# Ten rounds written out as straight code in place of a loop with six passes

## The chip, the cores and the metric

The kernel runs on one core of a Trainium2 chip. The metric is the device time of one execution, in microseconds. The core has five instruction streams that run side by side: TensorE (PE in the profile; its weight loads are listed apart as PEld), VectorE (DVE), ScalarE (ACT), GpSimd (POOL) and SyncE (SP), which here only starts transfers. They wait for one another through semaphores. A name with a q behind it (DVEq, PEldq) is the part of an engine that handles instructions before the work proper: register arithmetic, branches, waits, starts of transfers.

## The reference

The input x has 8 x 2048 tokens of 256 numbers, all float32. A layer norm is followed by a linear attention without a softmax, then a second layer norm and a mixture of experts with a short convolution:

```python
x = x + attn(layernorm(x), wq, wk, wv, wo)       # context = Q (K^T V) * sqrt(3/64), out = context wo^T, per sequence
x2 = layernorm(x)
scores = sigmoid(x2 @ Wr)                        # 8 experts
_, idx = top_k(scores + router_bias, 2)
w = scores[idx] / (sum + 1e-09)                  # spread over 8 columns as cw
hid = silu(x2 @ Wg[e]) * (x2 @ Wu[e])            # e = 0..3
routed = sum_e cw[:, e] * (hid @ Wd[e]) + (cw[:, 4] + cw[:, 6]) * x2 + cw[:, 7] * relu(x2)
x = x + routed + conv4(x2) + conv_b
```

## The kernel before

The 16384 tokens are 32 groups of 512 tokens (four tiles of 128), four groups to a sequence. Every group passes through stages, and each stage works on another group at the same time. One **step** of the program does stage L (load and first norm) for group s, stage A (transposes, and the Gram matrix of the normed rows) for group s-1, B (attention output, residual, second norm) for s-5, R (router) for s-6, C (experts) for s-7, and Y (output) for s-8; the table `LAG` holds these distances. A **round** is four steps, ten rounds are 40 steps, numbered 0 to 39 here. In the second step of a round stage B begins a new sequence, and a chain of small products (`ps_gram`, lines 518 to 545) folds the Gram matrix into one 256 x 256 matrix. Each product of the experts and of the attention is made as three matmuls of split operands (lines 371 to 373).

The order in each engine's stream is written by hand in its `body(st)`. The class `Step` decides which stages are on in a step and computes the number that each wait needs (`before`). The function `steps` calls `body`: rounds 0 and 1 and rounds 8 and 9 are written out with constants (*peeled*). Rounds 2 to 7, where all stages are on, are one copy of four steps in a hardware loop (`Fori`, line 295) with the round number in a register; the numbers for waits are then computed on each engine by register instructions. SyncE's loop ends one round earlier. Every engine goes through its own loop, and there is no barrier at a round's end.

Places of which the prediction speaks: in DVE's body line 938 (or 936) copies three columns ahead of the transposed group, the first VectorE work of a step; line 803 is the convolution, line 898 makes `x2T_lo`. TensorE's router matmuls (line 476) wait for `x2T_lo`, and TensorE works strictly in the order written. POOL's line 1059 is the router's exponential, line 1042 scales an expert's gate. PE's line 511 transposes the router's weights once in each step with stage R (steps 6 to 37), late in the step. The instructions of the loop itself all carry line 295.

Of the kernel before, what the change touches and what calls it, by code (L numbers as in the profile page):

```python
# [33 lines left out]
LAG = {"I": -1, "L": 0, "A": 1, "X": 4, "B": 5, "R": 6, "C": 7, "Y": 8}  # L34
UNROLL = 4
# [4 lines left out]
class Step:  # L40


    def __init__(self, r, s, groups):
        self.r, self.s, self.groups = r, s, groups
        self.peeled = isinstance(r, int)

    def on(self, stage):

        return not self.peeled or 0 <= UNROLL * self.r + self.s - LAG[stage] < self.groups

    def was_on(self, stage):


        return not self.peeled or 0 <= UNROLL * self.r + self.s - 1 - LAG[stage] < self.groups

    def later(self, stage, n):

        return not self.peeled or UNROLL * self.r + self.s - LAG[stage] >= n

    def first(self, stage):  # L60

# [10 lines left out]

    def before(self, stage, per=1, extra=0):

        n = self.s - LAG[stage]
        if self.peeled:
            return per * min(max(UNROLL * self.r + n, 0), self.groups) + extra
        return self.r * (UNROLL * per) + (n * per + extra)

    def uses(self, stage, n, per=1, extra=0):  # L80

# [3 lines left out]
    def chains(self, per=1, extra=0):  # L85


        k = (self.s - LAG["B"] - 1) // UNROLL + 1
        if self.peeled:
            return per * min(max(self.r + k, 0), self.groups // UNROLL) + extra  # L90
        return self.r * per + (k * per + extra)

    def chain(self):
        return self.first("B") and self.on("B")
# [6 lines left out]
def program(nc, x, wq, wkT, wvT, woT, wr, rbias, wg, wu, wd, convwb, cw_rows, out):  # L101
    T, H = x.shape
    D = wq.shape[0]
    NE = wr.shape[1]
    EM, _, I = wg.shape
    KC = convwb.shape[1] - 1
    HC = H // P
    TG = 4
    GT = TG * P
    NG = T // GT  # L110
    SCALE = math.sqrt(3.0 / D)
    assert D == 64 and I == P and HC == 2 and NG % UNROLL == 0
    ROUNDS = (NG + max(LAG.values())) // UNROLL
    LOOP = (LAG["Y"] // UNROLL, NG // UNROLL)

    x_rows = x.rearrange("(n p) f -> p n f", p=P)
    out_rows = out.rearrange("(n p) f -> p n f", p=P)
# [2 lines left out]
    with ctx:  # L120
# [166 lines left out]
        N_LOADS = 7 + 2 * EM + 1  # L287
        NSPLIT = 3

        def steps(eng, body, stop=LOOP[1]):  # L290

            for r in range(LOOP[0]):
                for s in range(UNROLL):
                    body(Step(r, s, NG))
            with eng.Fori(LOOP[0], stop, 1) as r:
                for s in range(UNROLL):
                    body(Step(r, s, NG))
            for r in range(stop, ROUNDS):
                for s in range(UNROLL):
                    body(Step(r, s, NG))  # L300

# [3 lines left out]
        @block.sync  # L305
        def _(sp):
            def load_x(st):

                if st.later("I", 2):
                    sp.wait_ge(xn_ready, st.before("I", TG, -TG))  # L310
                sp.dma_start(xa[:, st.slot("I", 2)], x_rows[:, bass.ds(st.group("I") * TG, TG), :])\
                    .then_inc(xa_loaded[st.slot("I", 2)], 16)

            load_x(Step(0, -1, NG))
            load_x(Step(0, 0, NG))
            sp.dma_start(wq_sb[:, :], wq).then_inc(w_loaded, 16)
            sp.dma_start(wkT_sb[:, :, :], wkT.rearrange("(c p) d -> p c d", p=P)).then_inc(w_loaded, 16)
            sp.dma_start(wvT_sb[:, :, :], wvT.rearrange("(c p) d -> p c d", p=P)).then_inc(w_loaded, 16)
            sp.dma_start(woT_sb[:, :], woT).then_inc(w_loaded, 16)
            sp.dma_start(wr_sb[:, :, :], wr.rearrange("(c p) e -> p c e", p=P)).then_inc(w_loaded, 16)  # L320
            sp.dma_start(conv_w[:, :, :], convwb.rearrange("(c p) k -> p c k", p=P)).then_inc(w_loaded, 16)
            sp.dma_start(bias8[:, :], rbias.partition_broadcast(P)).then_inc(w_loaded, 16)
            for e in range(EM):
                sp.dma_start(wg_st[:, e], wg[e].rearrange("(c p) i -> p c i", p=P)).then_inc(w_loaded, 16)
                sp.dma_start(wu_st[:, e], wu[e].rearrange("(c p) i -> p c i", p=P)).then_inc(w_loaded, 16)
            sp.dma_start(wd_st, wd.rearrange("e i n -> i e n")).then_inc(w_loaded, 16)

            def body(st):
                if st.on("I") and not (st.peeled and st.group("I") < 2):
                    load_x(st)  # L330
                if st.on("Y"):

                    k = st.slot("Y", 4)
                    for h in range(2):
                        sp.wait_ge(out_ready, st.before("Y", 2, h + 1))
                        sp.dma_start(out_rows[:, bass.ds(st.group("Y") * TG + 2 * h, 2), :],
                                     acc[:, k, 2 * h:2 * h + 2]).then_inc(out_stored[k], 16)
                if st.on("R"):

                    k = st.slot("R", 2)  # L340
                    rows = cw_rows[bass.ds(st.group("R"), 1)]
                    sp.wait_ge(cwT_ready, st.before("R", 1, 1))
                    sp.dma_start(rows.rearrange("a e (t n) -> (a e t) n", t=TG), cwT[:, :]).then_inc(cw_stored, 16)
                    sp.wait_ge(cw_stored, st.before("R", 16, 16))


                    if st.peeled and st.before("R") < 2:
                        sp.wait_ge(whi_ready, NSPLIT)
                        sp.wait_ge(wlo_ready, NSPLIT)
                    sp.dma_start(cwb[:, k].rearrange("p e n -> p (e n)"),  # L350
                                 rows.rearrange("a e n -> (a e n)").partition_broadcast(P))\
                        .then_inc(cwb_loaded[k], 16)
                if st.on("X"):

                    k = st.slot("X", 4)
                    if st.later("X", 4):
                        sp.wait_ge(out_stored[k], st.uses("X", 4, 32))
                    sp.dma_start(acc[:, k], x_rows[:, bass.ds(st.group("X") * TG, TG), :])\
                        .then_inc(acc_loaded[k], 16)

            steps(sp, body, LOOP[1] - 1)
            for k in range(4):
                sp.wait_ge(out_stored[k], 32 * (NG // 4))
            sp.wait_ge(cw_stored, 16 * NG)
# [3 lines left out]
        def _(pe):  # L368
# [182 lines left out]
            def body(st):  # L551
                c_on, y_on, r_on, a_on, b_on, m_on = (st.on("C"), st.on("Y"), st.on("R"), st.on("A"), st.on("B"),
                                                      st.chain())
                if st.peeled and b_on and st.before("B") == 0:
                    pe.wait_ge(w_loaded, 16 * N_LOADS)
                if st.peeled and c_on and st.before("C") == 0:
                    pe.wait_ge(wlo_ready, NSPLIT)
                if c_on:
                    gate_up(st, 0)
# [53 lines left out]
                if a_on and r_on:  # L613
                    xn_transpose(st, 1)

            steps(pe, body)


        @block.scalar
        def _(act):  # L620
# [36 lines left out]
            def split_weights():  # L657
                act.wait_ge(w_loaded, 16 * N_LOADS)
                copy(wgu_hi[:, 0].rearrange("p e c i -> p (e c i)"), wg_st.rearrange("p e c i -> p (e c i)"))\
                    .then_inc(whi_ready, 1)  # L660
                copy(wgu_hi[:, 1].rearrange("p e c i -> p (e c i)"), wu_st.rearrange("p e c i -> p (e c i)"))\
                    .then_inc(whi_ready, 1)
                copy(wd_hi[:, :, :], wd_st).then_inc(whi_ready, 1)
# [26 lines left out]

            def body(st):
                c_on, r_on, m_on = st.on("C"), st.on("R"), st.chain()
                if st.peeled and st.group("L") == LAG["B"] - 1:
                    split_weights()
                if m_on:
                    chain_copy(st, gram_done, st.before("A"),
# [67 lines left out]
                if st.on("B"):  # L764
                    norm2(st)

            steps(act, body)


        @block.vector  # L770
        def _(dve):
# [152 lines left out]

            def body(st):
                c_on, y_on, r_on, b_on, m_on = st.on("C"), st.on("Y"), st.on("R"), st.on("B"), st.chain()
                if st.peeled and st.group("L") == LAG["B"]:
                    split_weights()
                if r_on:
                    q = st.slot("R", 2)  # L930
# [38 lines left out]
                if c_on:  # L969

                    dve.wait_ge(relu_ready, st.before("C", TG, TG))
                    k = st.slot("C", 4)
# [25 lines left out]
            dve.wait_ge(iota_ready, 1)  # L998
            v.tensor_copy(iota_f[:, :], iota_u[:, :]).then_inc(iotaf_ready, 1)
            dve.wait_ge(iotaf_ready, 1)  # L1000
            steps(dve, body)


        @block.gpsimd
        def _(pool):
# [38 lines left out]
            def hid_low(st, e):  # L1044

                pool.wait_ge(hidhi_ready, st.before("C", EM, e + 1))
                g.tensor_tensor(hid_lo[:, 1], hid[:, 1], hid_hi[:, 1].bitcast(F32), ALU.subtract)\  # L1047
                    .then_inc(hidlo_ready[1], 1)

            def body(st):  # L1050
# [19 lines left out]
                                 st.before("B", 2, 2), rstd2_ready, st.before("B", 1, 1), shift2_ready)  # L1070
                if c_on:
                    hid_low(st, 3)
            steps(pool, body)


# [35 lines left out]
```

## Time and profile before

| quantity | value |
|---|---|
| time, median of 3 runs | 1014.47 us (1012.42 to 1015.83) |
| profiled execution: time, span | 1023.05 us, 1021.3 us |
| PE busy, share of the span | 944.8 us, 93% |
| DVE busy | 807.6 us, 79% |
| POOL busy | 560.1 us, 55% |
| ACT busy | 506.2 us, 50% |
| data moved | 86.64 MB in 60987 packets, mean 85 GB/s |
| mean granted TensorE clock | 0.953 of full speed |
| instructions in the span | 18818 |

The span goes from the first to the last instruction. The busy times are summed over the span. A granted clock of 1.00 is TensorE's level of 2.4 GHz and 0.50 is its level of 1.2 GHz; a mean between them is a stretch with both.

### The profile page before, as it was taken

How to read it: one execution, taken by the hardware profiler on the slowest of the kernel's cores; microseconds unless marked ns; L12 is line 12 of the kernel's file. 1: busy time of each engine (PE TensorE's matmuls, PEld its weight loads, DVE VectorE, ACT ScalarE, POOL GpSimd, SP SyncE). 2: the span in 40 equal slices, each digit the busy share in tenths (PEclk: the TensorE clock that was granted, in tenths of full speed). 3: DMA queues.
4: the chain of work that ended last, by engine and by line, in shares of the span. 5: the costliest groups of instructions: out<-in, count | busy, mean ns of one | idle time of the engine just before them, and what ended most of it. 6: DMA issues, size and time to landing. Idle time of an engine off the chain costs nothing.

```text
span 1021.3 us, 18818 instructions
## 1 busy us (share of the span) xinstructions
PE 944.8 (93%) x5816; PEld 828.5 (81%) x5816; DVE 807.6 (79%) x2294; ACT 506.2 (50%) x1003; POOL 560.1 (55%) x491
## 2 busy tenths in 40 slices
PE   4779999979999799997999979999899999988886
PEld 4568978968898688987888978988789898777775
DVE  6657878977689778996878968996888987777875
ACT  3455546544456454553555535555356554444342
POOL 2136656646566366664556655565566664565653
PEclk9779979998799899998999979999799999999999
DMA  5321222221222221223312222222022222122111
GB/s 175 104 76 51 80 86 104 104 84 51 73 103 103 83 76 48 103 103 104 103 62 83 79 86 103 103 97 89 21 103 103 83 83 83 63 83 83 63 49 56
DMA packets 60987, 86.64 MB, mean 85 GB/s; under 512 B 4480, under 2 KB 56832, under 8 KB 56832
## 3 DMA queue, kind: packets, MB, share of 16 engines
q1 hardware_dynamic: 60928, 86.01, 24.2%
q8 instruction: 17, 0.28, 0.1%
q14 instruction: 42, 0.34, 0.1%
HBM read 68.96 MB, written 17.04 MB: 84 GB/s over the span
## 4 chain that ended last, share of the span: by engine, by line
PE 58%; DVE 11%; issue 11%; POOL 10%; ACT 4%; DMA 3%; SPq 1%; POOLq 0%; DVEq 0%; ACTq 0%
PE ps_gu L371 8%; PE ps_gu L373 7%; PE ps_gu L372 7%; PE ps_sh L476 5%; POOL enx L1059 4%; PE ps_y L371 4%; PE ps_y L372 4%; PE ps_y L373 4%; PE ps_gram L435 3%; POOL gate L1042 3%; PE ps_y L419 2%; PE ps_sh L371 2%; PE ps_sh L372 2%; PE ps_sh L373 2%; POOL rstd L1024 2%
## 5 line engine op out<-in xcount | busy, mean ns | idle before, releaser
L1042 POOL TENSOR_TENSOR gate<-gate,cwb 128x512 f32<-128x512 f32 x128 | 176.6, 1380 | 207.4 <-ACT gate L629 127.8
L371 PE MATMUL ps_gu<-x2T_hi,wgu_hi 128*128 128x512 f32 x512 | 218.1, 426 | 2.3 <-DVE hid L786 2.3
L373 PE MATMUL ps_gu<-x2T_hi,wgu_lo 128*128 128x512 f32 x512 | 208.4, 407 | 0.0
L372 PE MATMUL ps_gu<-x2T_lo,wgu_hi 128*128 128x512 f32 x512 | 208.3, 407 | 0.0
L1059 POOL TENSOR_TENSOR enx<-inv_e,logits 128x32 f32<-128x32 f32 x32 | 184.8, 5773 | 42.2 <-ACT logits L622 42.1
L629 ACT ACTIVATE gate<-ps_gu 128x512 f32<-128x512 f32 x128 | 75.9, 593 | 178.5 <-PE ps_gu L373 178.5
L371 PE MATMUL ps_y<-wd_hi,hid_hi 128*128 128x256 f32 x512 | 153.3, 299 | 4.0 <-POOL hid_lo L1047 3.5
L803 DVE SCALAR_TENSOR_TENSOR conv<-x2T,conv_w,conv 128x512 f32<-128x512 f32 x192 | 147.0, 805 | 0.1
L372 PE MATMUL ps_y<-wd_lo,hid_hi 128*128 128x256 f32 x512 | 144.9, 283 | 0.0
L373 PE MATMUL ps_y<-wd_hi,hid_lo 128*128 128x256 f32 x512 | 144.8, 283 | 0.0
L371 PEld LDWEIGHTS ps_gu<-x2T_hi,wgu_hi 128*128 128x128 f32 x512 | 100.7, 197 | 24.3 <-DVE hid L786 6.3
L373 PEld LDWEIGHTS ps_gu<-x2T_hi,wgu_lo 128*128 128x128 f32 x512 | 100.2, 196 | 23.9
L786 DVE TENSOR_TENSOR hid<-ps_gu,gate 128x512 f32<-128x512 f32 x128 | 86.4, 675 | 33.9 <-PE ps_gu L373 26.4
L372 PEld LDWEIGHTS ps_gu<-x2T_lo,wgu_hi 128*128 128x128 f32 x512 | 100.7, 197 | 14.7
L1021 POOL TENSOR_TENSOR mv<-mv,eps_ln 128x4 f32<-128x4 f32 x64 | 12.7, 199 | 179.3 <-DVE mv L835 151.7
L1047 POOL TENSOR_TENSOR hid_lo<-hid,hid_hi 128x512 fp32r<-128x512 f32 x64 | 98.9, 1546 | 16.2 <-ACT hid_hi L622 16.2
L371 PEld LDWEIGHTS ps_y<-wd_hi,hid_hi 128*128 128x128 f32 x512 | 98.3, 192 | 6.8 <-POOL hid_lo L1047 4.6
L622 ACT ACTIVATE hid_hi<-hid 128x512 fp32r<-128x512 f32 x128 | 80.1, 626 | 47.7 <-DVE hid L786 45.2
L372 PEld LDWEIGHTS ps_y<-wd_lo,hid_hi 128*128 128x128 f32 x512 | 97.9, 191 | 1.4
L476 PEld LDWEIGHTS ps_sh<-wr_sb,x2T 128*128 128x128 f32 x512 | 69.8, 215 | 33.7 <-DVE x2T_lo L898 29.2
L373 PEld LDWEIGHTS ps_y<-wd_hi,hid_lo 128*128 128x128 f32 x512 | 96.9, 189 | 0.0
L476 PE MATMUL ps_sh<-wr_sb,x2T 128*128 128x8 f32 x512 | 69.3, 271 | 28.9 <-DVE x2T_lo L898 28.9
(94 smaller groups left out, 1974.5 us busy)
## 6 DMA issues: line engine op xcount, KB each, us to landing
cwb<-cw_rows SPq DMA_DIRECT2D x32, 1024.0 KB, 4.7
xa<-in_x SPq DMA_DIRECT2D x32, 512.0 KB, 6.5
acc<-in_x SPq DMA_DIRECT2D x32, 512.0 KB, 5.8
out<-acc SPq DMA_DIRECT2D x64, 256.0 KB, 2.2
cwb<-in_wg SPq DMA_DIRECT2D x4, 128.0 KB, 2.8
cwb<-in_wu SPq DMA_DIRECT2D x4, 128.0 KB, 2.8
cwb<-in_wd SPq DMA_DIRECT2D x1, 512.0 KB, 4.9
cw_rows<-cwT SPq DMA_DIRECT2D x32, 8.0 KB, 1.4
```

The lines of the kernel that those rows point to most:

```text
L371: nc.tensor.matmul(dst, a_hi, b_hi, start=start, stop=False, skip_group_check=True)
L372: nc.tensor.matmul(dst, a_hi, b_lo, start=False, stop=False, skip_group_check=True)
L373: return nc.tensor.matmul(dst, a_lo, b_hi, start=False, stop=stop, skip_group_check=True)
L435: nc.tensor.matmul(ps_gram[:, 0:H], xn[:, q, t, 0:P], xn[:, q, t, :], start=start, stop=stop, skip_group_check=True)
L476: last = nc.tensor.matmul(b[:, t * NE:(t + 1) * NE], x2T[:, q, c, PAD + t * P:PAD + (t + 1) * P], wr_sb[:, c], start=(c == 0), stop=(c == ...
L622: return nc.scalar.activation(dst, src, ACT.Copy, scale=scale)
L629: nc.scalar.activation(gate[:, e % 2], ps_gu[GU_BANK[2 * e]][:, :], ACT.Silu)\
L786: v.tensor_tensor(hid[:, e % 2], ps_gu[GU_BANK[2 * e + 1]][:, :], gate[:, e % 2], ALU.mult)\
L803: v.scalar_tensor_tensor(conv[:, c], x2T[:, q, c, k:k + GT], conv_w[:, c, k:k + 1], conv[:, c], ALU.mult, ALU.add).then_inc(conv_ready, 1)
L1042: g.tensor_tensor(gate[:, e % 2], gate[:, e % 2], cwb[:, q, e], ALU.mult).then_inc(gatew_ready, 1)
L1047: g.tensor_tensor(hid_lo[:, 1], hid[:, 1], hid_hi[:, 1].bitcast(F32), ALU.subtract)\
L1059: g.tensor_tensor(enx[:, :], inv_e[:, :], logits[:, :], ALU.pow).then_inc(enx_ready, 1)
```

## The change

The loop is taken out. `steps` calls `body` for all ten rounds with the round as a number, on every engine, and all numbers in waits are constants. Line numbers fall by some 5 to 12. The diff, cut to its core (the rest drops the tests on `peeled` and the engine argument of `steps`):

```diff
     def on(self, stage):
-        return not self.peeled or 0 <= UNROLL * self.r + self.s - LAG[stage] < self.groups
+        return 0 <= UNROLL * self.r + self.s - LAG[stage] < self.groups
...
     def before(self, stage, per=1, extra=0):
-        n = self.s - LAG[stage]
-        if self.peeled:
-            return per * min(max(UNROLL * self.r + n, 0), self.groups) + extra
-        return self.r * (UNROLL * per) + (n * per + extra)
+        n = UNROLL * self.r + self.s - LAG[stage]
+        return per * min(max(n, 0), self.groups) + extra
...
-        def steps(eng, body, stop=LOOP[1]):
-
-            for r in range(LOOP[0]):
-                for s in range(UNROLL):
-                    body(Step(r, s, NG))
-            with eng.Fori(LOOP[0], stop, 1) as r:
-                for s in range(UNROLL):
-                    body(Step(r, s, NG))
-            for r in range(stop, ROUNDS):
+        def steps(body):
+
+            for r in range(ROUNDS):
                 for s in range(UNROLL):
                     body(Step(r, s, NG))
```

VectorE's program before, at the end of the loop's body. A row is an instruction: line, operation, output and inputs, shape, and the semaphores it waits for. The row that follows in time, when the branch is taken, is the first of the second fence:

```order
L782 REGISTER_ALU [waits gatew_ready]
L786 TENSOR_TENSOR hid<-ps_gu,gate 128x512 [waits hidlo_ready1,gu_done]
L994 REGISTER_ALU
L995 TENSOR_TENSOR xnT_lo<-ps_sh,xnT_hi 128x512 [waits xnThi_ready]
L994 REGISTER_ALU
L995 TENSOR_TENSOR xnT_lo<-ps_sh,xnT_hi 128x512 [waits xnThi_ready]
L295 REGISTER_ALU
L295 COMPARE_AND_BRANCH
```

```order
L295 UNCONDITIONAL_BRANCH
L295 ISA
L934 ISA [waits x2T_ready]
L938 COPY x2T<-x2T 128x2x3 [waits conv_ready]
L940 ISA
L800 REGISTER_ALU [waits halo_ready]
L803 SCALAR_TENSOR_TENSOR conv<-x2T,conv_w,conv 128x512 [waits tap_ready] x2
L808 ISA
```

(The unconditional branch is passed on entry; the branch back goes to the row behind it.) The same place in the changed program, between round 2 and round 3:

```order
L774 TENSOR_TENSOR hid<-ps_gu,gate 128x512 [waits hidlo_ready1,gu_done,gatew_ready]
L983 TENSOR_TENSOR xnT_lo<-ps_sh,xnT_hi 128x512 [waits xnThi_ready] x2
L926 COPY x2T<-x2T 128x2x3 [waits conv_ready,x2T_ready]
L791 SCALAR_TENSOR_TENSOR conv<-x2T,conv_w,conv 128x512 [waits tap_ready,halo_ready]
L791 SCALAR_TENSOR_TENSOR conv<-x2T,conv_w,conv 128x512 [waits tap_ready]
L801 BN_STATS stats<-xa 128x6 [waits shift1_ready,xa_loaded0]
L801 BN_STATS stats<-xa 128x6 x3
```

No work is moved against other work; the register rows and the branch are gone, and what the loop held once stands in the program six times. TensorE's program at its loop's end before (the rows of the branch and of the round's last and next work):

```order
L451 MATMUL ps_sh<-ident,xn 128x128 [waits cwT_ready,xn_ready]
L451 MATMUL ps_sh<-ident,xn 128x128 x3
L295 REGISTER_ALU
L295 COMPARE_AND_BRANCH
L371 MATMUL ps_gu<-x2T_hi,wgu_hi 128x512 [waits gate_ready,x2Tlo_ready]
```

and after:

```order
L439 MATMUL ps_sh<-ident,xn 128x128 [waits cwT_ready,xn_ready]
L439 MATMUL ps_sh<-ident,xn 128x128 x3
L359 MATMUL ps_gu<-x2T_hi,wgu_hi 128x512 [waits gate_ready,x2Tlo_ready]
```

Here too the matmuls keep their order. Counted over the whole program, the written rows grow from 2018 to 5234 on PE, 968 to 2168 on DVE, 451 to 1005 on ACT, 240 to 495 on POOL and 155 to 210 on SP. (The weight load that goes with each matmul is not a row of its own, nor is the extra wait of an instruction that waits for two semaphores.) The loop's body held 707 of these rows on PE, 413 on DVE, 201 on ACT and 104 on POOL; 52, 143, 74 and 43 of them were register or other control rows, which are gone.

## Rows read from the trace of the kernel before

**Rows 1.** Span and mean granted clock of the core.
```profile
core 0: 1021.3 us, clock 0.953
```
**Rows 2.** Waits: engine, line, releaser; us in total, times, longest us.
```profile
DVE x2T L938 <- issue: 17.1, 3, 6.0
...
DVE x2T L938 <- ACT x2T L622: 10.5, 2, 5.3
...
PE ps_sh L476 <- DVE x2T_lo L898: 28.9, 7, 5.8
```
**Rows 3.** Line 295, 460 to 472 us: duration ns, first and last start us.
```profile
L295 PEldq COMPARE_BRANCH  x1: 208/208/208, 461.8 to 461.8; - x1
L295 PEldq FUSED_REGOPS  x1: 50/50/50, 462.1 to 462.1; - x1
...
L295 DVEq COMPARE_BRANCH  x1: 63/63/63, 464.3 to 464.3; - x1
L295 ACTq COMPARE_BRANCH  x1: 45/45/45, 464.4 to 464.4; - x1
...
L295 ACTq FUSED_REGOPS  x1: 50/50/50, 464.6 to 464.6; - x1
L295 DVEq FUSED_REGOPS  x1: 63/63/63, 469.9 to 469.9; - x1
```
**Rows 4.** Chain that ended last, 464 to 479 us: start, us, what.
```profile
464.36 5.59 issue
...
475.18 3.58 PE ps_sh L476 x16
```
**Rows 5.** Line 511 on PE, whole span: its 32 starts mark the steps.
```profile
L511 PE MATMUL ps_sh<-ident,cw x32: 269/273/277, 68.3 to 990.6; 128*16 128x128 f32 x32
```
**Rows 6.** Stretches from one line 511 to the next: busy times, clock, DMA share, GB/s.
```profile
core 0: us, PE busy (x) PEld busy (x) DVE busy (x) ACT busy (x) POOL busy (x), PEclk, DMA share, GB/s
96.15:123.03 26.88, 26.88 (x180) 24.44 (x177) 23.45 (x71) 15.46 (x30) 17.05 (x15) 1.00 0.28 99
123.03:158.67 35.64, 35.50 (x198) 29.45 (x196) 26.82 (x77) 17.05 (x36) 17.16 (x15) 0.86 0.22 75
213.12:249.75 36.63, 31.13 (x180) 27.55 (x178) 25.21 (x74) 15.29 (x30) 19.19 (x15) 0.86 0.21 72
249.75:285.05 35.30, 35.30 (x199) 29.44 (x197) 25.46 (x76) 17.02 (x36) 17.17 (x15) 0.85 0.22 75
339.12:375.89 36.77, 31.27 (x179) 27.64 (x177) 26.30 (x74) 15.28 (x30) 19.12 (x15) 0.86 0.20 72
375.89:406.55 30.66, 30.66 (x198) 26.41 (x196) 26.10 (x75) 17.03 (x36) 17.17 (x15) 1.00 0.24 86
460.88:496.30 35.42, 30.26 (x180) 27.04 (x178) 25.01 (x74) 15.29 (x30) 18.20 (x15) 0.90 0.22 75
496.30:528.46 32.16, 32.16 (x199) 27.11 (x197) 26.09 (x75) 17.02 (x36) 17.20 (x15) 0.95 0.24 82
582.58:618.57 35.99, 30.84 (x179) 27.46 (x177) 25.05 (x74) 15.28 (x30) 18.71 (x15) 0.86 0.22 74
618.57:649.23 30.66, 30.66 (x198) 26.42 (x196) 26.09 (x74) 17.03 (x36) 17.17 (x15) 1.00 0.25 86
703.32:740.76 37.44, 31.57 (x179) 27.85 (x177) 25.97 (x74) 15.29 (x30) 18.66 (x15) 0.86 0.21 71
740.76:771.42 30.66, 30.66 (x198) 26.41 (x196) 26.10 (x75) 17.03 (x36) 17.17 (x15) 1.00 0.23 86
771.42:798.30 26.88, 26.88 (x180) 24.43 (x177) 22.81 (x68) 15.35 (x30) 17.16 (x15) 1.00 0.28 98
...
825.62:852.54 26.92, 26.92 (x179) 24.42 (x177) 22.61 (x63) 13.44 (x26) 15.31 (x11) 1.00 0.22 79
```
**Rows 7.** DMA queues in the stretch behind the loop, 829 to 1021.3 us.
```profile
q8 instruction: 8, 0.13, 0.3%
q14 instruction: 7, 0.06, 0.1%
```

More of the change, by code:

```diff
@@ L44, in __init__ @@
         self.r, self.s, self.groups = r, s, groups
-        self.peeled = isinstance(r, int)
     def on(self, stage):
-        return not self.peeled or 0 <= UNROLL * self.r + self.s - LAG[stage] < self.groups
+        return 0 <= UNROLL * self.r + self.s - LAG[stage] < self.groups
     def was_on(self, stage):
-        return not self.peeled or 0 <= UNROLL * self.r + self.s - 1 - LAG[stage] < self.groups
+        return 0 <= UNROLL * self.r + self.s - 1 - LAG[stage] < self.groups
     def later(self, stage, n):
-        return not self.peeled or UNROLL * self.r + self.s - LAG[stage] >= n
+        return UNROLL * self.r + self.s - LAG[stage] >= n
     def first(self, stage):
@@ L88, in chains @@
         k = (self.s - LAG["B"] - 1) // UNROLL + 1
-        if self.peeled:
-            return per * min(max(self.r + k, 0), self.groups // UNROLL) + extra
-        return self.r * per + (k * per + extra)
+        return per * min(max(self.r + k, 0), self.groups // UNROLL) + extra
     def chain(self):
@@ L113, in program @@
     ROUNDS = (NG + max(LAG.values())) // UNROLL
-    LOOP = (LAG["Y"] // UNROLL, NG // UNROLL)
     x_rows = x.rearrange("(n p) f -> p n f", p=P)
@@ L328, in body @@
             def body(st):
-                if st.on("I") and not (st.peeled and st.group("I") < 2):
+                if st.on("I") and st.group("I") >= 2:
                     load_x(st)
@@ L344, in body @@
                     sp.wait_ge(cw_stored, st.before("R", 16, 16))
-                    if st.peeled and st.before("R") < 2:
+                    if st.before("R") < 2:
                         sp.wait_ge(whi_ready, NSPLIT)
@@ L359, in body @@
                         .then_inc(acc_loaded[k], 16)
-            steps(sp, body, LOOP[1] - 1)
+            steps(body)
             for k in range(4):
@@ L553, in body @@
                                                       st.chain())
-                if st.peeled and b_on and st.before("B") == 0:
+                if b_on and st.before("B") == 0:
                     pe.wait_ge(w_loaded, 16 * N_LOADS)
-                if st.peeled and c_on and st.before("C") == 0:
+                if c_on and st.before("C") == 0:
                     pe.wait_ge(wlo_ready, NSPLIT)
@@ L614, in body @@
                     xn_transpose(st, 1)
-            steps(pe, body)
+            steps(body)
         @block.scalar
@@ L692, in body @@
                 c_on, r_on, m_on = st.on("C"), st.on("R"), st.chain()
-                if st.peeled and st.group("L") == LAG["B"] - 1:
+                if st.group("L") == LAG["B"] - 1:
                     split_weights()
@@ L765, in body @@
                     norm2(st)
-            steps(act, body)
+            steps(body)
         @block.vector
@@ L926, in body @@
                 c_on, y_on, r_on, b_on, m_on = st.on("C"), st.on("Y"), st.on("R"), st.on("B"), st.chain()
-                if st.peeled and st.group("L") == LAG["B"]:
+                if st.group("L") == LAG["B"]:
                     split_weights()
@@ L1000, in _ @@
             dve.wait_ge(iotaf_ready, 1)
-            steps(dve, body)
+            steps(body)
         @block.gpsimd
@@ L1072, in body @@
                     hid_low(st, 3)
-            steps(pool, body)
+            steps(body)
 def kernel(**inputs):
```

## The prediction

> **What bounds the kernel now.** I read the mean clock first, then the list of waits, then the loop's own instructions, and last the stretches from step to step. The mean granted clock is 0.953 over a span of 1021.3 us [rows 1], so on a part of the span TensorE is at its lower level, although nothing in the program changes its work from round to round. The waits show where: VectorE's line 938, its first work in a step, sat idle for 27.6 us in five spells (17.1 in 3 that nothing explains, 10.5 in 2 that the list puts down to an ACT copy), and TensorE's router waited 28.9 us for `x2T_lo` [rows 2]. Five is the number of times that a loop with six passes branches back. The loop's instructions say that it is the branch: on VectorE it takes 63 ns at 464.3 us, and the next instruction of the loop comes at 469.9, some 5.6 us later. On ScalarE the same distance is 0.2 us, on TensorE 0.3 [rows 3]. The copy was done long before, so the list's second releaser is only the last event that it could find. The chain of waits has 5.59 us of "issue" there, and behind it the router's matmuls take 3.58 us for 16 [rows 4].
>
> The steps give the price. From one line 511 to the next is one step (32 starts, 68.3 to 990.6 us [rows 5]). The first steps of rounds 3 to 7, the ones behind a branch back, last 36.63, 36.77, 35.42, 35.99 and 37.44 us, with mean clocks of 0.86 to 0.90 [rows 6]. Two steps are the same work without a branch back: the first of round 2, which is entered from above (26.88 us at clock 1.00), and the first of round 8, which is behind the loop's end and has constants in its waits (26.92 us, clock 1.00; only the load and first norm are off in it) [rows 6]. In both PE is busy throughout, so a clean step is bound by TensorE. In the step at 213 us PE is idle for 36.63 - 31.13 = 5.50 us, and busy 4.25 us longer than in a clean one, which is the lower clock after the idle spell.
>
> **The change part by part.**
>
> *The five branches back.* The sum of the five first steps is 36.63 + 36.77 + 35.42 + 35.99 + 37.44 = 182.25 us. Clean ones would take 5 x 26.9 = 134.5. Gain 47.8 us, of which PE's idle time is 5.50 + 5.50 + 5.16 + 5.15 + 5.87 = 27.2 (stretch less PE busy, [rows 6]) and the clock 20.6. What is late next is PE itself, busy 26.88 of 26.88 us. Neither end is far off: at least the idle 27.2 must go with the branch, at most 47.8.
>
> *The steps behind those.* The second step of a round holds the chain for a new sequence, in which PE has little to do between short products that wait for ACT. It takes 30.66 us in rounds 4, 6 and 7 at clock 1.00, 32.16 in round 5, 35.30 in round 3 and 35.64 in round 2 [rows 6]. In round 2 no branch back came before it, and the clock was 0.86 all the same. So this drop is no child of the branch, and the change may leave it, remove it or add it. The five now sum to 35.30 + 30.66 + 32.16 + 30.66 + 30.66 = 159.44. If none drops, 153.3, a gain of 6.1; if all do as in round 2, 178.2, a loss of 18.8. I take the mean excess of the six cases over 30.66, (4.98 + 4.64 + 0 + 1.50 + 0 + 0) / 6 = 1.85: 5 x 32.5 = 162.6, a loss of 3.1.
>
> *The third and fourth steps* are already clean (26.88 us at 1.00, PE busy throughout [rows 6], and the others of their kind like it). Taken at 0.
>
> *The register instructions.* 143 control rows leave VectorE's body of four steps, 36 a step, 52 leave PE's. I cost them at nothing, because the step of round 8, with constants, takes 26.92 us and that of round 2, with registers, 26.88, and PE's matmuls cover both. The price of one such row is near the 50 to 63 ns of line 295's own [rows 3]: were the cover gone, 36 x 63 ns = 2.3 us a step on VectorE, 54 us over 24 steps, a bound from above on a further gain. The pair of steps lies at nothing, and so do I. A wait adds nothing and no queue is passed by another, since the order in every stream is kept.
>
> *The longer program.* It has to be brought to the engines. How much a block of instructions costs when it is late shows in the branch: 5.6 us. How much it costs when the code just runs on shows behind the loop: 8 + 7 blocks come in from 829 us on [rows 7], and VectorE's waits name no unexplained idle time outside of the branches back [rows 2]. I take 0; the other end is rival 3.
>
> The Trainium skill, in "Advanced Engine Details and Errata", section "Control Flow Timing", gives a compare-and-branch some 108 ns. The branch's own 63 ns on VectorE and 208 on PE [rows 3] are of that size, and by this rule alone the change would save 5 x 0.1 us and nothing else; the 5.6 us behind VectorE's branch contradict it as a price of the whole turn. The skill's "Runtime: NRT & Kernel Launch", section "Instruction fetch mechanics", says that a taken branch to a target outside the fetched window waits for a DMA, while straight code is fetched ahead and mostly hidden, and that TensorE's window is four times the others'. Its window of 512 instructions would put VectorE's 413 rows and their extra waits near the edge; no run here shows that number yet.
>
> *Sum.* -47.8 + 3.1 = -44.7 us. On the profiled execution: 1023.05 - 44.7 = 978.4 us. That execution was 8.6 us above the median of the runs shown (1014.47), and nothing in it says whether the branches are the reason. Off the median: 1014.47 - 44.7 = 969.8; if all of the 8.6 were in the branches' stalls, unprofiled runs would gain 36 and come to 978. I forecast 970.
>
> **The rivals.**
>
> *Rival 1: the clock takes much back.* Every chain step drops to the lower level as that of round 2 did, since the drop needs no branch. For it: rounds 2 and 3, one of them with no branch before it. Against: rounds 4, 6 and 7, and the stall, a stretch of idle TensorE, is gone. Then -47.8 + 18.8 = -29.0 us, 985 us.
>
> *Rival 2: the stall stays.* The pause at the branch is only where VectorE shows a wait that each round has anyway, so that straight code pauses at the same work. For it: the wait list names an ACT copy twice. Against: rounds 2 and 8 begin without a pause. Or the branch costs only what it shows itself. Time 1014 us, no change.
>
> *Rival 3: slower, the fetch becomes exposed.* Straight code on TensorE is 5234 rows in place of 2018, each matmul with its own load. The 8 blocks on q8 behind the loop go with PE's 989 rows there, some 1950 instructions with the loads, about 244 a block (an estimate: that q8 is PE's is inferred). The change adds 3216 rows, some 6400 instructions, 26 blocks. If each were waited for as VectorE's is at the branch, 26 x 5.6 = 146 us, and with the gain of 44.7 the time is 1014.5 - 44.7 + 146 = 1116. It decides from 44.7 / 26 = 1.7 us a block. Against it: a step of 26.88 us has 180 + 177 instructions on PE [rows 6], so 244 last 18 us, and a block takes no more than 5.6; also the peeled rounds show no such pause.
>
> *Rival 4: faster still.* The register rows were worth something in the chain steps and VectorE's gaps, and no chain step drops: -47.8 - 6.1 and some 10 of the 54 above, about 951 us.
>
> **How the numbers follow.** Forecast (958 to 981 us) 0.74; rival 1 0.12; rival 2 0.03; rival 3 0.05; rival 4 0.06. The range of 8 in 10 goes from 957 (clean everywhere: 1014.5 - 53.9 = 960.6, and a little of rival 4) to 988 (rival 1, and a smaller stall in unprofiled runs). Changes of 0.3%, some 3 us, are about what a measurement of this kernel can tell from none. Forecast and rivals 1 and 4 are faster by more: 0.92; rival 2 is the same: 0.03; rival 3 is slower: 0.05.
>
> **What would show each step.** On VectorE no idle spell of 5 us before the halo copy (now line 926). The first steps of rounds 3 to 7 at 26.9 us from one weights transpose to the next, clock 1.00. Chain steps at 30.7, or 35 where the clock falls: their count tells the forecast from rival 1. The round of the loop, 612.5 us for five, becomes 558 to 584. The instruction queues carry more blocks (q8 some 43 in place of 17), with no idle time of PE or VectorE that nothing explains. I am wrong if PE shows gaps of several us at places without a releaser, if the first steps stay above 30 us, or if steps that were clean (26.9) get longer.

## The result and the profile after

The straight program takes 970.59 us (median of 4 runs, 969.77 to 972.87) against 1015.04 us (4 runs) before: ratio 0.957, 95% interval 0.9546 to 0.9594. The forecast was 970. The profiled execution took 970.19 us, with a span of 968.4 us against 1021.3 [rows 1] and a mean granted clock of 0.983 against 0.953:

```profile
core 0: 968.4 us, clock 0.983
```

VectorE has no unexplained idle time left, and TensorE's router waits 2.6 us for `x2T_lo` where it waited 28.9 [rows 2]. The waits of the kernel after (engine, line, releaser; us in total, times, longest):

```profile
DVE x2T_lo L886 <- ACT x2T_hi L610: 24.4, 10, 4.8
DVE xnT_lo L983 <- ACT xnT_hi L610: 23.6, 34, 1.8
DVE acc L961 <- ACT x L721: 23.3, 32, 2.4
...
PE ps_sh L464 <- DVE x2T_lo L886: 2.6, 2, 1.6
```

Step by step, from one weights transpose (line 499 now) to the next, the rows that answer to [rows 6] (stretch; its length, PE, PEld, DVE, ACT and POOL busy, granted clock, DMA share, GB/s). They are the second step of round 2, both first steps of rounds 3 and 4 with the chain steps behind them, and the first step of round 7:

```profile
122.96:153.97 31.01, 30.88 (x198) 26.40 (x196) 26.80 (x76) 16.98 (x36) 17.18 (x15) 1.00 0.25 86
...
208.13:235.39 27.26, 27.13 (x180) 24.34 (x177) 25.45 (x72) 15.41 (x30) 17.09 (x15) 1.00 0.28 98
235.39:266.37 30.98, 30.86 (x199) 26.40 (x197) 26.78 (x76) 16.97 (x36) 17.16 (x15) 1.00 0.25 86
...
320.55:348.87 28.32, 27.40 (x179) 24.38 (x177) 26.11 (x74) 15.41 (x30) 18.09 (x15) 1.00 0.27 94
348.87:379.53 30.66, 30.66 (x198) 26.42 (x196) 26.08 (x75) 16.96 (x36) 17.15 (x15) 1.00 0.26 86
...
658.35:685.64 27.29, 27.17 (x179) 24.36 (x177) 25.48 (x72) 15.40 (x30) 17.12 (x15) 1.00 0.29 97
```

The first steps went from 35.4 to 37.4 us down to 27.3 (once 28.3), the second steps are at 31 us with the clock at 1.00 in each, and PE is busy nearly throughout. The steps that were clean before, third and fourth, did not change. The longer program shows in the instruction queues and nowhere else: q8 carries 46 blocks where the loop needed 17, q14 40 in place of 42.

```profile
q8 instruction: 46, 0.75, 0.3%
q14 instruction: 40, 0.33, 0.1%
```

### The profile page after: what moved, and what is told of

Same layout as the page of the kernel before. It is cut to its first block, busy times and chain, and to the rows that moved or that the text cites. A ratio compares the mean times of both kernels' runs of the same rounds, so it can differ in the third digit from the quotient of the medians.

```text
span 968.4 us, 16869 instructions
## 1 busy us (share of the span) xinstructions
PE 917.5 (95%) x5816; PEld 808.8 (84%) x5816; DVE 814.6 (84%) x2294; ACT 506.0 (52%) x1003; POOL 553.8 (57%) x491
## 4 chain that ended last, share of the span: by engine, by line
PE 55%; DVE 26%; ACT 6%; POOL 6%; issue 5%; DMA 1%; POOLq 0%; ACTq 0%; DVEq 0%
PE ps_gu L359 7%; PE ps_gu L361 7%; PE ps_gu L360 7%; PE ps_sh L464 5%; PE ps_y L359 4%; PE ps_y L360 4%; PE ps_y L361 4%; ACT x L676 4%; DVE stats L820 3%; POOL rstd L1012 3%; DVE acc L812 3%; PE ps_sh L454 2%; DVE chosen L863 2%; PE ps_y L407 2%; DVE hid L774 2%
## 5 line engine op out<-in xcount | busy, mean ns | idle before, releaser
L359 PE MATMUL ps_gu<-x2T_hi,wgu_hi 128*128 128x512 f32 x512 | 212.7, 415 | 0.8 <-DVE hid L774 0.8
L360 PE MATMUL ps_gu<-x2T_lo,wgu_hi 128*128 128x512 f32 x512 | 203.3, 397 | 0.0
L361 PE MATMUL ps_gu<-x2T_hi,wgu_lo 128*128 128x512 f32 x512 | 203.1, 397 | 0.0
L1047 POOL TENSOR_TENSOR enx<-inv_e,logits 128x32 f32<-128x32 f32 x32 | 177.1, 5533 | 7.2 <-ACT logits L610 7.0
L791 DVE SCALAR_TENSOR_TENSOR conv<-x2T,conv_w,conv 128x512 f32<-128x512 f32 x192 | 141.0, 773 | 0.0
L361 PEld LDWEIGHTS ps_gu<-x2T_hi,wgu_lo 128*128 128x128 f32 x512 | 97.3, 190 | 22.8
L359 PEld LDWEIGHTS ps_gu<-x2T_hi,wgu_hi 128*128 128x128 f32 x512 | 97.8, 191 | 20.6 <-DVE hid L774 4.7
L360 PEld LDWEIGHTS ps_gu<-x2T_lo,wgu_hi 128*128 128x128 f32 x512 | 97.6, 191 | 13.6
L610 ACT ACTIVATE hid_hi<-hid 128x512 fp32r<-128x512 f32 x128 | 80.1, 626 | 52.9 <-DVE hid L774 51.9
L423 PE MATMUL ps_gram<-xn 128*128 128x256 f32 x256 | 77.2, 384 | 0.0
L676 ACT ACTIVATE x<-acc,shift,rstd 128x256 f32<-128x256 f32 x128 | 66.4, 591 | 18.8 <-POOL shift L1014 18.8
## 6 DMA issues: line engine op xcount, KB each, us to landing
cwb<-cw_rows SPq DMA_DIRECT2D x32, 1024.0 KB, 4.7
```

The costliest lines, as they stand in the source:

```text
L359: nc.tensor.matmul(dst, a_hi, b_hi, start=start, stop=False, skip_group_check=True)
L360: nc.tensor.matmul(dst, a_hi, b_lo, start=False, stop=False, skip_group_check=True)
L361: return nc.tensor.matmul(dst, a_lo, b_hi, start=False, stop=stop, skip_group_check=True)
L423: nc.tensor.matmul(ps_gram[:, 0:H], xn[:, q, t, 0:P], xn[:, q, t, :], start=start, stop=stop, skip_group_check=True)
L610: return nc.scalar.activation(dst, src, ACT.Copy, scale=scale)
L676: nc.scalar.activation(x2[:, q, t], acc[:, st.slot("B", 4), t], ACT.Identity, bias=shift2[:, t:t + 1], scale=rstd2[:, t:t + 1]).then_inc(x ...
```

## The experiments

All change the kernel before. A time with a ratio is a median beside runs of the kernel before on the same chip; a time without one is a single profiled execution. "Pause" is the distance on an engine from the start of its closing branch to the next instruction of its loop.

**Which engine.** VectorE alone straight, and all but VectorE straight, by one more helper:

```diff
+        def straight(body):
+            for r in range(ROUNDS):
+                for s in range(UNROLL):
+                    body(Step(r, s, NG))
...
-            steps(dve, body)
+            straight(body)          # the second kernel: so for pe, act, pool and sp, not for dve
```

> Only VectorE's stream is written out; PE, ACT, POOL and SP keep the loop with register waits. Theory (the pause is VectorE's own, behind its branch back): all of the gain is there, 969 to 974 us, no idle spell of 5 us before line 938, first steps of rounds 3 to 7 at 27 us. Rival (the engines' loops share the cost, or the register instructions and branches of the other four engines matter): 980 to 1000 us. Rival (VectorE's branch costs nothing by itself, the pause is a wait): 1014 us.

> The opposite: PE, ACT, POOL and SP are straight code, VectorE keeps the loop. Theory: five pauses of 5.3 to 6.4 us on VectorE, first steps of rounds 3 to 7 at 35 to 37 us, 1010 to 1017 us, no better than before. Rival (the others' loops carry a part): 985 to 1005 us. If exposed fetching of PE's long program cost anything, this one would be slower than before.

With VectorE alone straight: 972.64 us, ratio 0.9565 (0.9537 to 0.9593), the whole gain. With all the others straight and VectorE looped: 1013.45 us, ratio 0.9971 (0.9945 to 0.9997), and VectorE's five pauses are there, in its waits as one row without an explanation:

```profile
DVE x2T L943 <- issue: 29.0, 5, 6.0
```

So the price is VectorE's alone. The second kernel also fetches the 46 blocks on q8 and is no slower than before, and the first keeps the 52 control rows of PE's loop, ACT's 74 and POOL's 43, and lies 2 us above the straight program, within the spread of either (969 to 973 in its unprofiled runs). Neither exposed fetching nor those register instructions cost anything that these runs can tell.

**A branch, or a branch back.** A loop of one pass around each of rounds 2 to 7:

```diff
-            with eng.Fori(LOOP[0], stop, 1) as r:
-                for s in range(UNROLL):
-                    body(Step(r, s, NG))
+            for k in range(LOOP[0], stop):
+                with eng.Fori(k, k + 1, 1) as r:
+                    for s in range(UNROLL):
+                        body(Step(r, s, NG))
```

> Straight code with a loop of a single pass around each of rounds 2 to 7 on every engine: an entry branch to the next row and a closing branch that is not taken, six times, and constants in all waits. Theory (only a taken branch back costs): 970 to 973 us, all first steps at 27 us. Rival (any branch interrupts the flow of instructions): about 1010 us.

972.49 us, ratio 0.9566 (0.9526 to 0.9607), first steps of rounds 3 to 7 at 26.9 to 27.8 us. Branches that stay in the stream cost nothing that these runs can tell; the jump back does.

**Turn or fetch.** VectorE's loop gets one instruction at its top that names the closing branch ahead of time. It is meant to have the branch's target at hand when the branch comes:

```diff
+        def loop(eng, stop):
+            if eng is not nc.vector:
+                return eng.Fori(LOOP[0], stop, 1)
+            return nc.Fori(LOOP[0], stop, 1, engines=bass.OrderedEngineSet([eng.engine]), hint_back_edge=True)
...
-            with eng.Fori(LOOP[0], stop, 1) as r:
+            with loop(eng, stop) as r:
```

> The loop as before on all engines, with one instruction more at the top of VectorE's body, which names the closing branch ahead of time so that its target can be brought in early. Theory (the pause is the fetch of the loop's first instructions, which left the engine's memory): the pause falls from 5.6 us to well under 1 us, 970 to 975 us with all register instructions still there. Rival (the pause is the turn itself, such as draining the engine or setting up registers): pauses stay at 5.6 us, 1015 us. Rival (register instructions cost a share of the 44 us): pause gone, but 980 us or more.

977.11 us, ratio 0.9622 (0.9584 to 0.966). All five pauses are gone (first steps of rounds 3 to 7 at 27.1 to 27.2 us), with all loops and register instructions in place, and q14 brings 17 blocks in place of 42: five fewer for each turn. Here is one turn on VectorE, then the instruction queues over the loop from 200 to 778 us (q14 has no row at all), and last those of the kernel before over a single pass, from 343 to 464 us:

```profile
L300 DVEq COMPARE_BRANCH  x1: 68/68/68, 325.9 to 325.9; - x1
L300 DVEq BRANCH_PREFETCH_HINT  x1: 39/39/39, 326.2 to 326.2; - x1
```
```profile
q1 hardware_dynamic: 35385, 53.36, 26.6%
q8 instruction: 1, 0.02, 0.0%
```
```profile
q14 instruction: 5, 0.04, 0.1%
```

So the announcement does not bring the target in from memory a little earlier: nothing is brought in, and the pass stays where it was. What is left above 972 is one new pause at the loop's end, where the announced branch isn't taken and the code behind it is late. The waits on VectorE, and the step at that place (the first of round 8, 26.92 us before [rows 6]):

```profile
DVE conv L808 <- issue: 4.6, 1, 4.6
```
```profile
771.37:805.05 33.68, 30.41 (x180) 27.10 (x178) 24.16 (x65) 13.31 (x26) 15.92 (x11) 0.90 0.18 63
```

This shows that the 5.6 us are waiting for instructions, not the work of turning. The new pause of 4.6 us makes its step 33.68 - 26.92 = 6.8 us longer, since the clock is at 0.90 in it.

**What sets a pause's length.** The same order of work, but VectorE's loop is cut in the middle of a step, ahead of the router's small operations:

```diff
+            body(Step(LOOP[0], 0, NG))                  # the part of a step ahead of route()
+            with dve.Fori(LOOP[0], LOOP[1] - 1, 1) as r:
+                for s in range(UNROLL):
+                    body_b(Step(r, s, NG))              # route() and what follows it
+                    body(Step(r, s + 1, NG))
```

> VectorE's loop is cut at another place: it begins ahead of the router's chain of small operations, in the middle of a step, when no load of cwb, acc or xa is running; the order of the work is the same. Five passes, so four turns. Theory (a pause's length is a fetch from memory that shares the DMA engines with the loads at a step's end): a pause of 2 to 4 us in place of 5.6, and 970.6 + 4 x 3 to 6 = 983 to 995 us. Rival (the length is the fetch's own): pauses of 5.5 us still, and 970.6 + 4 x 8.9 = 1006 us if PE waits as before, less if there is slack at that place.

983.34 us, ratio 0.9686 (0.9626 to 0.9746), with pauses of 2.85, 2.78, 2.77 and 2.75 us. Here is the first, and then the load of the DMA engines around it (second last column), against the share around the turn at 464 us in the kernel before:

```profile
L1013 DVEq COMPARE_BRANCH  x1: 63/63/63, 231.3 to 231.3; - x1
L1013 DVEq FUSED_REGOPS  x1: 63/63/63, 234.2 to 234.2; - x1
```
```profile
231.00:232.00 1.00, 1.00 (x9) 0.95 (x9) 0.95 (x2) 0.00 (x0) 1.00 (x1) 1.00 0.00 0
232.00:233.00 1.00, 1.00 (x9) 0.91 (x8) 0.00 (x0) 0.00 (x0) 0.92 (x4) 1.00 0.03 8
233.00:234.00 1.00, 1.00 (x6) 0.82 (x5) 0.00 (x0) 0.00 (x0) 0.92 (x2) 1.00 0.00 0
```
```profile
465.00:466.00 1.00, 1.00 (x6) 0.82 (x5) 0.00 (x0) 1.00 (x3) 0.49 (x1) 1.00 1.01 418
466.00:467.00 1.00, 1.00 (x10) 0.83 (x8) 0.00 (x0) 0.84 (x2) 0.00 (x0) 1.00 0.98 385
467.00:468.00 1.00, 1.00 (x10) 1.00 (x10) 0.00 (x0) 0.99 (x2) 0.00 (x0) 1.00 0.85 282
```

With the DMA engines idle the pause is half as long. The trace's list of packets says where the rest lies. Mid-step, the first 8 KB packet on q14 starts 0.9 us after the branch has ended, takes 0.4 to 0.5 us, and the next instruction comes 1.3 to 1.4 us behind it. In the kernel before, beside up to 2 MB of loads, the three parts are 3.7 to 4.4, 0.3 and 1.6 us: what grew is the wait for the packet's start. The time lost per turn fell further, to (983.3 - 970.6) / 4 = 3.2 us against (1015.0 - 970.6) / 5 = 8.9: in the first step of round 4 PE is busy 27.32 of 28.71 us at clock 1.00, so the lower clock is not paid there (two of the chain steps behind have 0.95). Here place and DMA load change together, and also PE's slack; the next kernel turns at the old place before the loads have begun.

**Fewer turns, longer passes.** Two rounds a pass, so two turns:

```diff
-            with eng.Fori(LOOP[0], stop, 1) as r:
-                for s in range(UNROLL):
+            with eng.Fori(LOOP[0], LOOP[0] + 2 * ((stop - LOOP[0]) // 2), 2) as r:
+                for s in range(2 * UNROLL):
```

> The loop's body holds two rounds, so there are three passes and two turns in place of five. In the trace of before a pass is 469 instructions on VectorE, 251 on ACT, 107 on POOL and some 1550 on PE; here it is twice that. Theory (each turn costs about 9 us, whatever the body's length, where it doesn't fit): VectorE alone pausing gives 970.6 + 2 x 8.9 = 988 us. If PE's body of some 3100 no longer fits either, PE pauses at the same two turns: its pause and VectorE's overlap in part, 988 to 1000 us. Rival (the cost grows with what must be fetched again): the pause is longer than 6.4 us, above 1000 us.

983.81 us, ratio 0.9655 (0.9605 to 0.9705; one run of 3156.79 us is left out of it). That is a little under the 988 us expected at least. PE now pauses as well, 3.8 and 3.4 us, ahead of VectorE (3.0 and 3.9) and ACT (2.5 and 4.1); the line's rows at the first turn:

```profile
L295 PEldq COMPARE_BRANCH  x1: 3755/3755/3755, 324.1 to 324.1; - x1
...
L295 DVEq COMPARE_BRANCH  x1: 63/63/63, 326.5 to 326.5; - x1
...
L295 DVEq FUSED_REGOPS  x1: 63/63/63, 329.5 to 329.5; - x1
```

PE's pause is inside its branch (3755 ns in place of 208 [rows 3]). A turn costs (983.8 - 970.6) / 2 = 6.6 us. The pauses of three engines lie beside each other. At the first turn the large load was issued only at 327.5 us, and the packet for VectorE starts at 327.6, again 0.9 us after its branch, at the place in the step where it took 3.7 us or more beside the loads: so it is the load that makes the pause long, not the place. At the second turn the load was issued at 556.6 us, just ahead of VectorE's branch at 556.7, and the packet starts after 1.9 us.

**How long may a pass be.** Three kernels change a pass's length, each executed once. ACT's pass in the kernel before has 249 records in the trace from one closing branch to the next, 255 by the program's rows; VectorE's has 467 and 471. (The 251 and 469 of the expectations are not what the trace has.) The first kernel leaves out the router's small operations on VectorE (two stand for twenty); the second adds 20 idle instructions at four places of ACT's looped step, the third five at each step's start.

```diff
-                done(v.tensor_scalar(den[:, :], enx[:, :], 1.0, None, ALU.add))
...
+                v.tensor_copy(cw[:, q].rearrange("p e t -> p (e t)"), enx[:, :]).then_inc(cw_ready, 1)
+                dve.wait_ge(cw_ready, st.before("R", 1, 1))
+                v.tensor_tensor(coef[:, q], cw[:, q, EM], cw[:, q, EM + 2], ALU.add).then_inc(rt, RT)
```
```diff
+            def pad(st):
+                for _ in range(0 if st.peeled else 20):          # 5 in the third
+                    act.nop("pad")
```

> The router's 20 small operations on VectorE are left out (two stand in their place), so the output's expert weights are wrong; VectorE's pass falls from 469 to some 265 instructions, all loops stay. Theory (a pass must be short enough for the engine's instruction memory, the limit between 251 and 469): VectorE's next instruction comes within 0.3 us of the branch, all first steps at 27 us or under. Rival (VectorE's turn costs 5.6 us whatever the body): five pauses as before.

> 80 idle instructions a step (four places of 20) are added to ACT's looped body, its pass grows from 251 to 571. Theory (length decides, on any engine): ACT now pauses some 5 to 6 us at each of five turns, beside VectorE's, where before it had 0.2 us. The time rises by the idle instructions' own cost and little by the pauses, which lie beside VectorE's: 1015 to 1040 us. Rival (the pause is a peculiarity of VectorE): ACT's distance from branch to next instruction stays 0.2 to 0.3 us.

> Five idle instructions a step on ACT; its looped pass has 275 instructions by the program's rows in place of 255. So far: passes of 255 on ACT do not pause, passes of 323 and 471 on VectorE and 571 on ACT do. (Of the short router's pass I had written 265; by the program's rows and by the trace it is 323.) Theory A (a fixed limit near 256): ACT now pauses 5 to 6 us at each turn. Theory B (a limit between 275 and 323, or one set by where the pass lies in blocks of fetched instructions): ACT's turn stays at 0.2 to 0.3 us. Time 1000 to 1016 us either way, since VectorE still pauses.

A fourth also leaves out two of the three convolution taps and the norm statistics of three of four tiles on VectorE, to come to 243; beside the short router:

```diff
+                if n > 0:                                        # in conv_tap
+                    return
...
-                for t in range(TG):
-                    v.bn_stats(stats1[:, t], xa[:, q, t]).then_inc(stat1, 1)
+                v.bn_stats(stats1[:, 0], xa[:, q, 0]).then_inc(stat1, TG)
```

> VectorE's pass cut to 243 instructions, below ACT's that does not pause: the router's small operations, two of the three convolution taps and three of four tiles' norm statistics are left out, so the output is not the reference's. Theory (the pass's length decides, on any engine): no pause behind VectorE's branch, 0.3 us; first steps of rounds 3 to 7 at 27 us; 960 to 972 us with the loops of all engines in place. Rival (something else about VectorE's turn): five pauses of 5.6 us, 1000 to 1010 us.

The first has 323 instructions a pass, not the 265 of my expectation, which forgot repeated rows and second waits. It pauses 5.6 to 5.9 us at every turn (1007.92 us). ACT with 571 pauses 5.6 to 6.2 us at every turn, so it is no peculiarity of VectorE (1004.07 us, less than the kernel before although two engines pause; its first steps are 34.4 to 35.0 us, and why, no run tells). ACT with 275 doesn't pause: 0.2 to 0.3 us (1016.65 us). The kernel named for 243 has 251 records a pass in the trace, and doesn't pause either: 0.3 us, first steps of rounds 3 to 7 at 26.9, 937.1 us with all loops in place (960 to 972 expected), but also with less work. A limit at 256 is ruled out by ACT's 275 (270 in the trace), and one by count would lie between 275 and 323. But the count is not what decides. The short router again, and then the kernel before itself, with VectorE's loop begun at the start of a block of fetched instructions:

```diff
+            return nc.Fori(LOOP[0], stop, 1, engines=bass.OrderedEngineSet([eng.engine]), head_slot={eng.engine: 0})
```

> The kernel with the short router (VectorE's pass has 323 instructions, the output's expert weights are wrong), but the loop's first instruction on VectorE is placed at the start of a block of fetched instructions. The queue q14 brings blocks of about 8 KB, three of which hold a pass that begins at a block's start and three or four one that does not. Theory B (the engine keeps a few such blocks, one of them fetched ahead, and a pass that touches one too many loses its first): no pause here, 965 to 975 us. Theory A (a limit by the count of instructions, between 255 and 323): five pauses as before, 1005 to 1012 us.

> The kernel before with one thing changed: VectorE's loop begins at the start of a block of fetched instructions; the pass has its full 471 instructions, four blocks of 128 or two of 256. Aligned, the pass of 323 did not pause, and it did unaligned. Theory B1 (the engine holds four blocks of 128, one of them fetched ahead): 471 touches four and the fifth is ahead, so the pause stays, 1010 to 1016 us. Theory B2 (room for 512 instructions and nothing taken away ahead of time): no pause, and 970 to 975 us with loops and registers on all engines, as fast as the straight program.

The short router's pass of 323, now begun at the start of a block, turns without a pause: 955.45 us against 1007.92, below the 965 to 975 expected. The lines of the loop on VectorE around one turn, first with its head anywhere, then with it aligned, and last the aligned kernel's queue (14 blocks in place of 39):

```profile
L295 DVEq COMPARE_BRANCH  x1: 63/63/63, 328.5 to 328.5; - x1
L295 DVEq FUSED_REGOPS  x1: 63/63/63, 334.1 to 334.1; - x1
```
```profile
L300 DVEq COMPARE_BRANCH  x1: 67/67/67, 319.7 to 319.7; - x1
L300 DVEq FUSED_REGOPS  x1: 63/63/63, 320.1 to 320.1; - x1
```
```profile
q14 instruction: 14, 0.11, 0.0%
```

The full pass of 471 keeps its five pauses (5.8 to 6.1 us) when aligned and gets a sixth on entry, where the jump to the aligned head now leads over padding: step 8 takes 36.83 us where it took 26.88. The time is 1024.01 us, ratio 1.0082 (1.0051 to 1.0114), 0.8% slower than before. The medians differ by 1024.0 - 1016.8 = 7.2 us, the profiled step 8 by 9.95. B2 is refuted. Theory B1, four blocks of 128 of which one is fetched ahead, fits all eight cases, and the packets on q14 bear most of it out:

- *A block has 128 instructions.* With VectorE alone straight, one packet comes every 107 to 144 of its records (12 intervals between 219 and 742 us), 127 in the mean. On q8, whose packets have 16 KB, it is 256 of TensorE's (26 intervals in the straight program), where the forecast had worked out 244.
- *Where a pass lies.* In the kernel before the five packets of a pass start at 0, 7 to 10, 93, 217 and 339 records behind the branch. The last three, some 125 apart, mark the ends of blocks, so that the pass begins about 35 into a block, and 35 + 467 lies over four. The unaligned 323 has them at 0, 6, 10 or 11, 137 and some 266: it begins some 118 into a block, and 118 + 323 lies over four too. Aligned, it lies over three.
- *What stays.* A pass of 471 or 323 that pauses brings in five blocks each time, the four it lies over and one more; ACT's 571, whose blocks come on q14 too, brings in six (eleven a pass with VectorE's). The aligned 323 and the pass of 251 bring in none from the first turn to the last, and so does the announced 471.

Over which blocks ACT's 275 lay can't be told, since it brought none in. That the block fetched ahead is what drives out the first is inferred from these counts; shown is that the place decides, and that a pass which pauses is fetched again whole.

## Why the prediction was right

*The five branches back* (-47.8 us): right in mechanism and size. The five first steps sum to 27.26 + 28.32 + 27.29 + 27.28 + 27.29 = 137.44 us (five stretches of the kernel after, of which three are shown above), 44.8 less than the 182.25 before. I had set 26.9 a step from round 2's and round 8's; these have 27.3, once 28.3, and why they are longer was not looked into. The term came out 3.0 short.

*The chain steps* (+3.1 us): wrong in sign in these two profiles. They went from 159.44 to 154.47, a gain of 5.0, and round 2's own, which I had left as it was, from 35.64 to 31.01, 4.6 more. I reasoned that the drop of round 2 had no branch before it, so that straight code would keep dropping now and then. Over the second steps of rounds 2 to 7, the clock was below 1.00 in 8 of 48 in the eight profiles with pauses at turns, and in 1 of 36 in the six without, so the pausing kernels have most of the drops. But two of the eight are those of the loop cut mid-step, where the clock falls 1.7 to 2.0 us into the step, just behind the pause. The other six, and the one of a kernel without pauses, all fall 12.7 to 13.9 us into the step, in the chain, and three of them in round 2, ahead of any turn (35.64, 32.52 and 34.09 us). For rounds 3 to 7 that leaves 3 of 40 against 1 of 30, too few to call the pauses the cause. What makes the drops in the chain stays open, and so does how much of the 9.6 us gained there belongs to the change and how much to chance. Rival 1, a drop in every chain step, is refuted.

*Register instructions* (0) and *the longer program* (0): right, as the first two experiments show. The announced loop confirms it: 977.1 less the 6.8 us of its step with the new pause is 970.3, with every register instruction in place. q8 has 46 blocks, 43 had been worked out. Rival 3 is refuted. Of rival 4 one half came true, that no chain step of rounds 3 to 7 drops; the other did not, there was nothing to gain from the register rows.

*Profile and median.* Measured in profiles the gain is 52.9 us of span, in medians 44.5. I had left open whether the profiled execution's extra 8.6 us before lay in the pauses. It does not have to: three of its chain steps dropped to the lower clock for 4.98 + 4.64 + 1.50 = 11.1 us, while the profiled execution of the kernel with all but VectorE straight, with the same pauses and one such drop, took 1017.29 us. So the forecast came out at 970 in part by luck, because two errors cancelled. Against the sum of -44.7 the profile gained 8.2 us more (8.1 from the chain steps and 4.6 from round 2's, less 3.0 in the first steps and some 1.5 elsewhere), and the profiled execution before was 8.6 us above its median, mostly by those same drops.

*Rival 2* is refuted by the kernel with VectorE alone straight. The Trainium skill's ~108 ns for a compare-and-branch ("Advanced Engine Details and Errata", section "Control Flow Timing") is between what the branch back itself takes here, 45 to 90 ns on ACT and VectorE and 207 to 243 on PE where PE does not pause, and misses what may stand behind it. "Runtime: NRT & Kernel Launch", section "Instruction fetch mechanics", has the mechanism right: a target outside of the fetched window waits for a DMA. Its 512 instructions agree with the announced pass of 471, which stayed in whole, but they are not what an ordinary pass may have here: 323 paused or not by its place, 471 paused in either place. For TensorE it states 2048; passes of 1529 records didn't pause and those of 3037 and 3049 did, which agrees.

## What to carry to other kernels

Look for a row "issue" on one line that comes once per pass of a loop, and compare each engine's distance from its closing branch to the next instruction: one engine with a long body can stall all the others, and straight code on that engine alone repairs it. If the loop must stay, shorten that engine's pass, announce the branch, or cut the loop where the DMA engines are idle and the others have slack; check the entry and the exit too. A pause of 5.6 us in front of the bounding engine costs more than itself, here 8.9 us, since TensorE's clock falls to its lower level after it. Some 10 us behind the branch at 464.3 us, for example, it stands at 0.50 for 6.8 us:

```profile
474.87:481.70 6.83, 6.52 (x23) 5.89 (x24) 6.03 (x11) 0.77 (x2) 2.63 (x1) 0.50 0.22 77
```

## What the runs showed that was not expected

- Where a pass begins decides whether it pauses: 323 instructions took 0.3 us a turn in one place and 5.6 to 5.9 in another, 52 us over the kernel (one execution each).
- At a turn that pauses, five blocks more come in on q14, whether the pass has 471 instructions (42 blocks against 17 with the branch announced, five turns) or 323 (39 against 14). The passes that turn freely bring in none at all.
- The announced branch moved the pause to the loop's exit (4.6 us), and aligning the head added one of 6.6 us at the entry (its step is 9.95 us longer): in both, the code that runs next wasn't there.
- The pause is 2.8 us with idle DMA engines and 5.6 to 6.4 beside the kernel's loads, and the difference is the wait for the first packet's start.
